# Wide cross attention: the value product moved behind the weighted values in TensorE's order

## The reference

```python
B, N, _ = q.shape                 # 8, 100
M = kv.shape[1]                   # 361
qh = (q @ Wq).reshape(B, N, 16, 64).transpose(0, 2, 1, 3)
kh = (kv @ Wk).reshape(B, M, 16, 64).transpose(0, 2, 1, 3)
vh = (kv @ Wv).reshape(B, M, 16, 64).transpose(0, 2, 1, 3)
scores = jnp.einsum('bhnd,bhmd->bhnm', qh, kh) * scale
attn = jax.nn.softmax(scores, axis=-1)
out = jnp.einsum('bhnm,bhmd->bhnd', attn, vh)
out = out.transpose(0, 2, 1, 3).reshape(B, N, 1024)
return out @ Wo + bo
```

## Time and profile before

| | |
|---|---|
| median of 3 runs | 3356.46 us |
| the three runs | 3343.63, 3356.46, 3372.39 us |
| the profiled execution: its time, its span | 3355.4 us, 3353.6 us |
| PE busy | 2989.9 us (89% of the span) |
| DVE busy, ACT busy | 1463.8 us (44%), 742.3 us (22%) |
| wide steps | about 1062 us to 1385 us of the span |

### The profile page before, as it was taken

How to read it: one execution, slowest core, us unless ns; L and a number is a source line. 1 busy time by engine, 2 the same in 40 slices (tenths; PEclk the granted TensorE clock), 3 DMA queues, 4 the chain that set the end, 5 groups by cost and what they waited for, 6 DMA issues and landing times.

```text
span 3353.6 us, 62701 instructions
## 1 busy us (share of the span) xinstructions
PE 2989.9 (89%) x25725; PEld 1713.2 (51%) x25725; DVE 1463.8 (44%) x3531; ACT 742.3 (22%) x1835; POOL 215.6 (6%) x393
## 2 busy tenths in 40 slices
PE   5878889789978888899979979999999999999587
PEld 3554456579754444555545643444444444444277
DVE  3645345311256455400365432455555555555622
ACT  2331133211122444311013411111111111111110
POOL 3001110020201000000200000000000000000011
PEclk9889989699989999899979969999999999999799
DMA  4000000359300000401000048000000000000086
GB/s 141 1 1 1 12 9 2 127 187 330 124 26 1 1 1 1 136 32 44 1 1 1 2 124 251 16 17 21 20 17 19 20 16 21 21 17 20 29 278 209
DMA packets 78764, 192.77 MB, mean 57 GB/s; under 512 B 32478, under 2 KB 54731, under 8 KB 67180
## 3 DMA queue, kind: packets, MB, share of 16 engines
q1 hardware_dynamic: 74524, 184.17, 16.9%
q0 software_dynamic: 4096, 6.57, 0.7%
HBM read 161.29 MB, written 29.39 MB: 57 GB/s over the span
## 4 chain that ended last, share of the span: by engine, by line
PE 78%; DVE 11%; ACT 5%; issue 3%; POOL 2%; DMA 1%; another core or an unknown queue 0%; SPq 0%; POOLq 0%; DVEq 0%; ACTq 0%
PE banks L1154 31%; PE banks L979 8%; PE banks L816 4%; PE banks L539 4%; PE banks L1122 3%; PE banks L710 3%; PE banks L1043 2%; PE banks L1182 2%; PE banks L492 2%; PE banks L1055 2%; PE banks L838 2%; ACT arena L1359 2%; PE banks L856 1%; DVE peaks L1809 1%; PE banks L666 1%
## 5 line engine op out<-in xcount | busy, mean ns | idle before, releaser
L1154 PE MATMUL banks<-arena 128*32 128x384 f32 x12800 | 1032.2, 486 | 1.1 <-DVE arena L2069 1.1
L1154 PEld LDWEIGHTS banks<-arena 128*32 128x32 f32 x12800 | 431.9, 110 | 601.6 <-issue 599.6
L1493 ACT ACTIVATE arena<-arena 128x256 f32<-128x256 f32 x200 | 83.2, 416 | 753.8 <-DVE arena L2081 753.8
L2081 DVE TENSOR_TENSOR arena<-banks,arena 128x256 f32<-128x256 f32 x200 | 84.9, 424 | 294.5 <-PE banks L1154 294.5
L979 PE MATMUL banks<-arena 128*128 128x400 f32 x512 | 172.5, 499 | 1.5 <-DVE arena L2031 0.8
L816 PE MATMUL banks<-arena 128*100 128x256 f32 x512 | 149.0, 449 | 18.1 <-ACT arena L1417 5.4
L539 PE MATMUL banks<-XNT,arena 128*128 128x400 f32 x384 | 147.3, 525 | 8.3 <-ACT XNT L1246 3.7
L1235 ACT ACTIVATE arena<-banks 128x512 f32<-128x512 f32 (+2 forms) x120 | 68.6, 572 | 385.7 <-PE banks L1043 153.8
L710 PEld LDWEIGHTS banks<-arena 32*121 32x121 f32 x1536 | 106.9, 198 | 62.6 <-ACT arena L1337 46.9
L979 PEld LDWEIGHTS banks<-arena 128*128 128x128 f32 x512 | 97.1, 190 | 76.8 <-DVE arena L2031 1.4
L1693 DVE TENSOR_REDUCE arena<-banks 100x4 f32<-100x1444 f32 x64 | 106.3, 1661 | 63.6 <-PE banks L666 63.3
(11 more groups left out here) (310 smaller groups left out, 4032.7 us busy)
## 6 DMA issues: line engine op xcount, KB each, us to landing
arena<-fc SPq DMA_DIRECT2D x22, 1024.0 KB, 6.7
arena<-pj SPq DMA_DIRECT2D x22, 1024.0 KB, 5.2
arena<-gu SPq DMA_DIRECT2D x21, 1024.0 KB, 7.2
arena<-whh SPq DMA_DIRECT2D x32, 384.0 KB, 11.7
arena<-dn SPq DMA_DIRECT2D x21, 512.0 KB, 5.2
arena<-xw SPq DMA_DIRECT2D x408, 24.0 KB
xw<-arena SPq DMA_DIRECT2D x6, 1536.0 KB, 7.6
arena<-hh SPq DMA_DIRECT2D x16, 512.0 KB, 3.3
```

What stands on the lines that cost most here:

```text
L1154: last = nc.tensor.matmul(banks[32 * j:32 * j + 32, 2 * c + i, 0:384].rearrange("p (g n) -> p g n", g=3), hT[:, 1 - i, 32 * ub:32 * ub + 3 ...
L1493: nc.scalar.activation(rz[:, c, :], pre[:, c, :], ACT.Sigmoid).then_inc(sem["rz_done"], 1)
L2081: nc.vector.tensor_tensor(pre[:, c, :].rearrange("p (g n) -> p g n", g=2), banks[:, 2 * c + i, 0:2 * P].rearrange("p (g n) -> p g n", g=2) ...
```

## The change

In `wide_step` on PE, the block with the value product is taken from between the transposes of step p and the weighted values of step p - 1, and put behind the weighted values. Nothing else is edited; the programs of DVE, ACT, POOL and SP keep their instructions and their order. Since `open_m` is called in program order, the value product now asks for its bank after the weighted values have opened theirs (steps 1 and 5) or given it free (steps 0 and 4).

```diff
                     last.then_inc(sem["t_full"], 1)
-                j, v_ = at_(p + 8)
-                if 0 <= p + 8 < 8 * B and v_ < 6:
-                    c, half = v_ // 2, v_ % 2
-                    w, full_ = open_m(ph, "vW", j, v_)
-                    nc.tensor.matmul(w[0:EXACT[c][1] - EXACT[c][0], :], mem[ph]["ctx"][:, j % B, slice(*EXACT[c])],
-                                     wb("x_wv")[:, 512 * half:512 * half + 512], start=True, stop=True).then_inc(sem[full_], 1)
                 if 0 <= p - 1 < 8 * B:
                     j, u = at_(p - 1)
...
                     if u % 4 == 3:
                         last.then_inc(sem[wide_full[0]], 1)
                         held.clear()
+                j, v_ = at_(p + 8)
+                if 0 <= p + 8 < 8 * B and v_ < 6:
+                    c, half = v_ // 2, v_ % 2
+                    w, full_ = open_m(ph, "vW", j, v_)
+                    nc.tensor.matmul(w[0:EXACT[c][1] - EXACT[c][0], :], mem[ph]["ctx"][:, j % B, slice(*EXACT[c])],
+                                     wb("x_wv")[:, 512 * half:512 * half + 512], start=True, stop=True).then_inc(sem[full_], 1)
```

## The result

The changed kernel takes 3365.58 us (median of 20 runs, 3354.19 to 3383.86), the kernel before 3350.45 us (median of 20 runs, 3343.63 to 3372.39). The ratio is 1.0039 with a 95% interval of 1.0025 to 1.0054: slower by 13 us, somewhere between 8 and 18. Timed a second time beside the kernel before, it came out at 1.0033 (1.0011 to 1.0054). So the sign is that of the forecast, the time lies in its range, and the size is about twice the +6 us that were worked out. That the forecast time, 3362 us, lies within 4 us of the measured one is in part luck: it was built on the three-run median of 3356.5 us, which is 6 us above the 20-run median of the same kernel.

What follows compares the result with a forecast made beforehand. A loop over three engines, not one engine, was taken to bound the wide steps. Ordinary items +2.4, item 8 +0.2 and queries' work +3.4 gave +6.0 us on 3356.5, so 3362 us, with an 8-in-10 range of 3341 to 3383.

Steps and rivals of the forecast that it cites:

- steps 0 and 4: Wide steps where the value product must wait for ACT's copy of the weighted values: +0.15 us each (0.10 to 0.22).
- step 2: Wide step where the weighted values run inside the wait for the keys' copy, so scores come earlier: -0.67 us.
- step 3: Wide step followed by the output product, where the weighted values already hid behind DVE's copy: 0 us.
- steps 1 and 5, scores behind: Wide steps where the longer value product now stands between keys' copy and next scores: +0.38 us each.
- keys of step 6: Step 6 has no value product, but its keys may wait some 0.05 us for DVE's copy.
- steps 1 and 5, queries' work behind: Four places where queries' work follows and needs the value product's bank, waiting for DVE's copy: 0.85 us more each.
- an ordinary item: One item's wide steps between two output products: +0.4 us on 39.04, giving about 39.4 us.
- Rival (a): Value product waits only for the keys' copy; 0.67 us saved in steps 0, 2, 3, 4: 18 us, 3338; chance 0.08.
- Rival (b): DVE's copy of the value product holds up the maxima in 34 steps: up to +23 us, 3386; chance 0.06.
- Rival (c): PE's granted clock in the wide steps falls from 1.00 to 0.83: +36 us, 3398; chance 0.03.

Runs made afterwards that it cites:

- e1: Kernel before, with the value product put behind the weighted values in step 2 only (seven places): ratio 0.9999 (0.9988 to 1.0010).
- e2: Kernel before, with the value product put behind the weighted values in steps 1 and 5 only (14 places): ratio 1.0031 (1.0017 to 1.0045).
- e3: Kernel before, with the value product behind the weighted values in even steps only, keeping its old bank: ratio 0.9975 (0.9962 to 0.9988).
- e11: Changed kernel, with ACT's copy of the weighted values (steps 0 and 4) right behind the keys' copy: ratio to the kernel before 1.0008 (0.9991 to 1.0025).
- e10: Changed kernel plus an extra 600-column DVE copy behind value-product copies from step 16 on: profile only, wide steps +11.7 us against the kernel before.
- e4: Kernel before, with only the turn of the two shared banks flipped ahead of phase C: ratio 1.0004 (0.9993 to 1.0014).
- e7: Kernel before, with ACT copying the keys ahead of the exponentials: ratio 0.9869 (0.9836 to 0.9902).
- e12: Kernel before, with even-step value products behind the weighted values in their old bank and ACT copying keys ahead of the exponentials: ratio 0.9874 (0.9840 to 0.9909).
- e8: Changed kernel, with ACT copying the keys ahead of the exponentials: ratio to the kernel before 0.9983 (0.9961 to 1.0005).
- e6: Kernel before, with the value product of step 0 issued twice in six items, order and banks unchanged: ratio 1.0034 (1.0006 to 1.0063).

## Why the prediction was right, and where not

**The wide steps** came out as worked out, term by term:

| term | predicted | measured |
|---|---|---|
| step 2 | -0.67 | -0.67 |
| step 3 | 0 | 0 |
| steps 0 and 4 | +0.15 (0.10 to 0.22) | +0.10 |
| steps 1 and 5, scores behind | +0.38 | +0.38 |
| keys of step 6 | +0.05 | +0.07 |
| steps 1 and 5, queries' work behind | +0.38 + 0.85 | +1.23 to +1.29 |
| an ordinary item | 39.4 us | 39.40 us |
| sum | +6.0 | +6.1 (+5.7 at a like clock) |

What made this possible is that each new start is the end of one known row plus 0.05 or 1.05 or 1.90 us, read from rows of the same kind. e1 and e2 show two of the terms by themselves, e3 that the bank makes that of steps 0 and 4, e11 which copy it waits for. In step 3 the gain is swallowed by DVE's copy ahead of L816, which was the last link ahead of L816 already; its wait grew to 0.79 as foreseen (0.85). The terms that are a little off are those of steps 0 and 4: from its step's scores to the value product it is 4.22 us in place of 3.45, 0.77 later and not 0.85, and 0.67 of that is given back.

**Rival (a)**, that the banks don't bind, fell in the trace of the change and is what e3 builds for the even steps: where it holds, the order is worth 13.4 us. The 18 us that the prediction gave it count step 3 as well, where DVE's copy ahead of L816 keeps the gain from coming through. **Rival (b)** did not happen by a margin of 0.1 to 0.2 us; e10 shows what a copy longer by 0.38 us would cost, 0.18 to 0.19 us a place. Its price in the prediction is a little high: the 34 steps include the four behind which, by its own text, stands the queries' work and not scores, so 30 and 21 us. **Rival (c)** did not happen in the wide steps, whose mean clock stayed at 0.99 to 1.00 in all traces but e10's.

**What was missed** lies outside them. The prediction said that nothing in the change reaches another stretch, and put the whole at +6. The runs say +13 and +11, with 6.1 below the first interval (8 to 18 us) and inside the second (4 to 18). The stretch behind the wide steps can take anything from 717 to 735.5 us with the same instructions, by how much of it is granted the lower clock level. In single traces it took 720 to 722 us in before, e2, e4, e7, e12 and one of the two of the change, 729 to 735.5 in e1, e3, e8 and the other, and 717 to 725 in the rest. The exchanged banks are ruled out as a cause of 7 us (e4).

The timed runs show that the excess goes with the clock. Each is on record with its mean granted clock: 0.9370 on average over the 32 executions of the changed kernel (0.9363 in the first 20, 0.9383 in the other 12), 0.9393 over the 75 executions of the kernel before that were timed beside the experiments (0.9388 over the 29 of them beside those 12). A line through the times against span times (1 - clock), with an offset between the two kernels, puts that offset at +6.4 us (95% interval 5.2 to 7.8). This is an estimate, and good to a few us only: the same line puts e1 at -3, e3 at -11, e2 at +10, e6 at +8.5 and e8 at -12.5, where their wide steps say -4.8, -13.4, +9.1, +5.1 and -17. At the same clock, then, the changed kernel is slower by about what its wide steps show, and the rest of the 13 us is a lower granted clock.

Why its clock was lower is open. In e1, e3 and e8, three different kernels, the pieces at the lower level lie at the same distances behind the last scores, to 0.3 us, and the stretch takes 729.2, 728.9 and 728.9 us; so its length follows a pattern that comes back. Whether shifting that stretch in time, as any change of the wide steps does, picks the worse pattern more often, or whether 10 to 20 runs simply fell so, no run here settles: e6, made to tell, has an interval that holds both, and e1, e3 and e8 timed 4.5, 5 and 12 us worse than their wide steps and e12 3 us (with intervals of 4 to 12 us to either side) while e2, e4, e7 and e11 timed within 2. The mechanism was right for the wide steps; the size of the whole was right to within this spread and no better.

## What to carry to other kernels

- Where buffers are handed out in program order, moving a product also moves it to another buffer. Follow each wait to the semaphore and count that it gets in the new order before costing the order itself; e3 took the gain (0.67 us a step) only by keeping the bank.
- Hiding the short of two products in a wait and leaving the long one behind it is a loss when there is room for only one: compare what remains between the last wait and the next link (1.05 against 0.67 us in steps 1 and 5).
- An engine that waits on a loop over three is freed by cutting the loop, here by one copy on ACT that did not need to queue behind the exponentials (-44 us), not by permuting the waiting engine's queue.

## What the runs showed of the hardware

- Steps of the wide stage repeat to 0.01 us from kernel to kernel at the upper clock level, so that one trace resolves changes of 0.1 us that 20 timed runs of the whole cannot; the whole varies by some 30 us between executions (3342 to 3379 us over 75 of the kernel before).
- The same 735 or 721 us of instructions behind the wide steps, with mean clock 0.89 or 0.91, in two executions of one program: 14 us of PE's clock. Ahead of the wide steps the first 1050 us varied by 17 us (1049.6 to 1066.3) over the traces.
- The clock did not mind the waits: with PE idle for 1.36 us in step 0 and 1.43 in step 4 of the ordinary items, and for 0.5 to 0.6 us in four other steps, the windows of whole ordinary items still show 1.00. The Trainium skill (TensorE: Matmul & The Clock Gate, "A second HAM failure mode: psum-queue depth-cycling") tells of a kernel whose bank cycling made the clock swing; these wide steps, which cycle through two banks with such waits, do not show it: where a trace has pieces at the lower level in them at all, they lie in the first two items and make 3.4 to 10 us.
